# Mixture of experts on one core: all 64 experts in the fixed body, half tiles at other places, five of eight picks read back inside the loop

## The chip, the core and the metric

The kernel runs on one core of a Trainium2 chip. The metric is the device time of one execution in microseconds (us). The engines are TensorE (PE; its weight loads are listed as PEld), VectorE (DVE), ScalarE (ACT), GpSimd (POOL) and SyncE (SP, which here issues the plain DMAs; POOL issues the indirect ones). Each engine runs its own list of instructions in order and waits for the others by semaphores.

## The reference

One transformer block on X of 4 x 512 tokens with D = 512 columns in f32: a modulated layernorm, an attention (linear, without softmax over keys) with a residual, a second modulated layernorm, and a mixture of experts with a residual. The part that the change touches is the mixture. It is, cut to what matters:

```python
logits = x @ gate_w.T                              # 2048 tokens, 64 experts
topv, topi = jax.lax.top_k(logits, 8)
rw = softmax(topv)
W = zeros((N, 64)).at[arange(N)[:, None], topi].set(rw)
gu = einsum('nh,eih->nei', x, gu_w)                # gate and up: 512 -> 2 x 128
gate, up = gu[..., :128], gu[..., 128:]
inter_w = silu(gate) * up * W[:, :, None]
out = einsum('nei,ehi->nh', inter_w, dp_w)         # down: 128 -> 512, summed over experts
out = out + sigmoid(x @ sh_gate1_w.T) * shared_expert(x)
x = x + gb * out                                   # gb: a gate per batch entry
```

So each of 2048 tokens picks 8 of 64 experts, 16,384 pairs of a token and an expert, 256 an expert on average. The kernel computes an expert only on the tokens that picked it.

## The kernel before, in words

The first part (layernorms, attention, shared expert, routing) ends at about 360 us. In it POOL writes, by indirect DMA, for each expert the list of its pairs; the list of all experts lies in memory as `slots` and is read back into the table `tbl` (`load_table`): one column is the 128 pairs of one tile.

**The loop over experts.** The work is in tiles of 128 gathered tokens. Every expert has two fixed tiles (FIXED = 2). What an expert has beyond 256 tokens goes into half tiles of 64 rows; two halves, mostly of two experts, make up one tile of the kind `rest` (18 of them, `REST`). The order is written out by hand in `BODY` (L72 on), a list of tiles: experts 1 to 56 with two tiles each, and a half-tile pair after the tile numbers in `REST_AFTER` (after experts 11, 13, 15, 18 and so on, about every two and a half experts, up to expert 53). Experts 57 to 64 (`LISTED = 8`) are not in the body but in `laps` of four experts: two laps always (`OWN_LAPS`), more in a hardware loop if the routing needs them. In a lap the number of the expert and the column of the table are read from lists in memory (`plan`) on SP (`load_listed`), ACT (`own_listed`), DVE (`list_listed`) and POOL (`gather_listed`). 112 + 18 + 16 = 146 tiles are computed.

A `unit` is an expert's two tiles or one tile of halves. For each unit, in this order:

- SP loads the expert's weights, 768 KB, into one of four slots (`WSLOTS = 4`, `fixed_w`), when the down matmuls of the expert four earlier are done (`after_down`, L624). The weights of a tile of halves go into their own two slots (`rest_w`): gate and up 2 x 512 KB after the gate and up of the tile of halves before (`load_rest_gu`, L566; `next_rest_gu`, L617), down 2 x 256 KB after its down (`load_rest_down`).
- POOL gathers the 128 rows of the tile from memory (indirect DMA, L766, `gather`), eight tiles ahead, and after each gather scatters the results of the tile two earlier to `y_rows` (L775, `put_rows`), a row for each pair. Ids of a tile of halves come from DVE (`list_rest`, L1432: for each half it reads a column number from memory and copies the column).
- PE transposes the gathered rows of the next unit (L2016, `turn`), does gate and up (L2026, `gate_up`; halves L2037, `gate_up_rest`), and then the down matmuls of the unit before (L2046; halves two units later, L2054). ACT copies the transposed rows (L1006) and applies silu (L1016, halves L1014). DVE multiplies (the gating, L1622, halves L1620) and scales the results by the token's weight (L1641).
- In the first units DVE and PE also plan: they count the tokens of each expert, lay out the halves and write the lists (`plan_step` on PE, `take_over` to `plan_listed` on DVE, `lists`). DVE turns parts of the table into gather ids with `list_fixed` when it comes to tiles 6, 10 and 12.

**The final stage.** For each token the eight rows of `y_rows` are summed, scaled by gb and added to x. There are 16 groups of 128 tokens. Picks are sorted by expert, so a token's last picks in the order of the row are done earliest. Two picks (`EARLY = 2`) are read in the last lap (`read_early`, L663). The other six (`LATE = 6`) are read in halves of three rows, 768 KB each (`read_back`, L670), into five buffers (`BACK = 5`); the first ones that need all scatters go out after the last scatter has landed. PE sums four of the six late rows by matmuls with the identity into a bank (`late_row`, L2134; `BY_PE = 4`), DVE adds the other two (`late_pair`, L1703), the two early ones to each other (`early_pair`, L1699), then the bank's sum (L1718), scales (L1719) and adds to x (L1720), and SP stores the group.

## Time and profile before

| | |
|---|---|
| median of 3 runs | 967.36 us (964.57 to 973.53) |
| span of the profiled execution | 965.6 us |
| PE busy | 872.5 us (90%) |
| DVE busy | 465.5 us (48%) |
| POOL busy | 458.7 us (48%) |
| ACT busy | 214.3 us (22%) |
| moved by DMA | 221.36 MB, mean 229 GB/s |
| mean granted clock of PE | 0.970 of full speed |

The runs and the profile are different executions of the same kernel; the median stands 1.8 us above the span of the profiled one. The span is from the first to the last instruction. Busy shares are means over stages with different limits: PE is at nine tenths and more from about 430 us to the end of the loop, DVE is busiest in routing and in the final stage, and DMA moves more than 300 GB/s in most of the loop and about 400 in the final stage.

### The profile page before, as it was taken

The numbers are of one execution on the slowest core, as the hardware profiler recorded it, in microseconds if no ns is written. First come the engines' busy times: TensorE is split into PE (matmuls) and PEld (weight loads), VectorE is DVE, ScalarE is ACT, GpSimd is POOL, SyncE is SP. The second block draws the span as 40 slices with busy tenths as digits, with TensorE's granted clock in tenths as the row PEclk, the third lists the DMA queues.
The fourth block names the chain that finished last, engine by engine and source line by source line (L and its number), as shares of the span: only waits on it lengthen the run. The fifth ranks groups of instructions, "written<-read, shape, count | busy, mean of one in ns | idle before, by whom it ended". The sixth has DMA issues, their size and how long they took to land.

```text
span 965.6 us, 12358 instructions
## 1 busy us (share of the span) xinstructions
PE 872.5 (90%) x3437; PEld 514.2 (53%) x3437; DVE 465.5 (48%) x1177; ACT 214.3 (22%) x559; POOL 458.7 (48%) x447
## 2 busy tenths in 40 slices
PE   6999989989988694979989998999999999986997
PEld 2434534534534343657666665666666666763442
DVE  4797785788586540423323323333233333324496
ACT  2022221321312111212232222322223222321000
POOL 1420055236355766357556666566665656655000
PEclk9999999999998697989999999999999999998999
DMA  9951003103003152788898998889998997899997
GB/s 341 326 163 71 1 8 96 45 2 104 1 1 115 41 190 73 229 289 277 289 322 272 339 323 315 307 286 338 325 319 302 311 333 262 283 354 402 382 419 315
DMA packets 76927, 221.36 MB, mean 229 GB/s; under 512 B 19078, under 2 KB 19462, under 8 KB 76472
## 3 DMA queue, kind: packets, MB, share of 16 engines
q1 hardware_dynamic: 48760, 149.12, 43.9%
q0 software_dynamic: 28096, 71.42, 21.0%
q8 instruction: 29, 0.48, 0.2%
q14 instruction: 42, 0.34, 0.1%
HBM read 183.98 MB, written 48.87 MB: 241 GB/s over the span
## 4 chain that ended last, share of the span: by engine, by line
PE 60%; issue 8%; DVE 7%; another core or an unknown queue 7%; DMA 4%; SPq 3%; ACT 2%; ACTq 0%; POOL 0%; DVEq 0%; POOLq 0%
PE bank L2026 17%; PE bank L2046 8%; PE bank L1798 7%; PE bank L2016 5%; PE bank L1845 5%; PE bank L1911 3%; PE bank L2136 3%; DMA front<-y_rows 3%; PE bank L2037 2%; PE bank L1809 2%; SPq L668 2%; PE bank L2054 1%; PE bank L1930 1%; DMA front<-h_rows,gid_fixed 1%
## 5 line engine op out<-in xcount | busy, mean ns | idle before, releaser
L2026 PE MATMUL bank<-h2T,wqkv 128*128 128x256 f32 x1024 | 243.1, 388 | 9.9 <-issue 9.6
L719 POOL DMA_INDIRECT slot_table<-pair,place x128 | 130.4, 1019 | 183.3 <-DVE place L1262 118.2
L2026 PEld LDWEIGHTS bank<-h2T,wqkv 128*128 128x128 f32 x1024 | 193.1, 194 | 41.1 <-issue 16.5
L775 POOL DMA_INDIRECT y_rows<-front,tbl x110 | 113.6, 1033 | 83.8 <-DVE front L1641 38.1
L766 POOL DMA_INDIRECT front<-h_rows,gid_fixed x112 | 115.8, 1034 | 69.1 <-issue 31.6
L2046 PE MATMUL bank<-wqkv,front 128*128 128x512 f32 x256 | 127.9, 621 | 11.2 <-DVE front L1622 7.5
L1641 DVE TENSOR_SCALAR front<-bank,wgt 128x512 f32<-128x512 f32 x146 | 107.1, 748 | 43.3 <-DMA y_rows<-front,tbl 19.8
L1006 ACT ACTIVATE h2T<-bank 128x512 f32<-128x512 f32 x148 | 82.2, 595 | 161.4 <-issue 65.6
L1798 PE MATMUL bank<-wqkv,front 128*128 128x512 f32 x256 | 113.5, 594 | 0.0
L1622 DVE TENSOR_TENSOR front<-bank,front 128x256 f32<-128x256 f32 x64 | 27.2, 424 | 177.4 <-ACT front L1016 135.2
L2016 PEld LDWEIGHTS bank<-const,front 128*128 128x128 f32 x592 | 69.1, 143 | 62.0 <-issue 47.4
L2016 PE MATMUL bank<-const,front 128*128 128x128 f32 x592 | 81.6, 277 | 22.3 <-ACT h2T L1006 10.3
L2046 PEld LDWEIGHTS bank<-wqkv,front 128*128 128x128 f32 x256 | 44.2, 191 | 70.5 <-issue 33.5
L1798 PEld LDWEIGHTS bank<-wqkv,front 128*128 128x128 f32 x256 | 47.6, 190 | 55.9 <-issue 55.1
L1620 DVE TENSOR_TENSOR front<-bank,front 128x128 f32<-128x128 f32 x18 | 5.3, 292 | 113.3 <-ACT front L1014 96.2
L1845 PE MATMUL bank<-front 128*128 128x512 f32 x128 | 56.6, 594 | 2.5 <-DVE front L1252 2.4
L1809 PE MATMUL bank<-front,wqkv 128*128 128x512 f32 x128 | 58.2, 599 | 0.0
L1016 ACT ACTIVATE front<-bank 128x256 f32<-128x256 f32 x64 | 24.2, 378 | 143.5 <-PE bank L2026 64.5
L2136 PE MATMUL bank<-front,const 128*128 128x512 f32 x100 | 47.2, 622 | 6.9 <-DMA front<-y_rows 6.6
L1845 PEld LDWEIGHTS bank<-front 128*128 128x128 f32 x128 | 23.8, 190 | 31.5 <-issue 29.4
L1809 PEld LDWEIGHTS bank<-front,wqkv 128*128 128x128 f32 x128 | 23.6, 190 | 30.5 <-issue 30.5
L2136 PEld LDWEIGHTS bank<-front,const 128*128 128x128 f32 x100 | 19.3, 199 | 34.1 <-issue 20.8
(292 smaller groups left out, 860.1 us busy)
## 6 DMA issues: line engine op xcount, KB each, us to landing
wqkv<-in_experts SPq DMA_DIRECT2D x64, 768.0 KB
front<-in_experts SPq DMA_DIRECT2D x36, 512.0 KB
front<-y_rows SPq DMA_DIRECT2D x20, 768.0 KB, 12.4
front<-in_experts SPq DMA_DIRECT2D x36, 256.0 KB
wqkv<-y_rows SPq DMA_DIRECT2D x12, 768.0 KB, 13.4
front<-in_w_mod SPq DMA_DIRECT2D x5, 1024.0 KB, 10.1
x<-in_x SPq DMA_DIRECT2D x4, 1024.0 KB, 10.8
h_rows<-h SPq DMA_DIRECT2D x4, 1024.0 KB
```

The lines of the kernel that those rows point to most:

```text
L719: pool.indirect_dma_start(out=slots[:, :], out_offset=bass.IndirectOffsetOnAxis(ap=place[b % 2][:, i, k:k + 1], axis=0), in_=pair[:, b * T ...
L766: pool.indirect_dma_start(out=xg[s], out_offset=None, in_=h2_rows[:, :], in_offset=bass.IndirectOffsetOnAxis(ap=of, axis=0), bounds_check= ...
L775: pool.indirect_dma_start(out=y_rows[:, :], out_offset=bass.IndirectOffsetOnAxis(ap=to, axis=0), in_=yb[s], in_offset=None, bounds_check=P ...
L1006: sc.activation(xT[u % 2][:, :, i * P:(i + 1) * P], bank[n % 2][:, :].rearrange("p (k t) -> p k t", k=KC), ACT.Copy).then_inc(s_xT, 1)
L1641: ve.tensor_scalar(yb[n % YBUFS], bank[4 + n % 2][:, :], wgt[:, n % ROUND:n % ROUND + 1], None, ALU.mult).then_inc(s_y, 1)
L1798: mm = pe.matmul(bank[2 + j][:, :], hT[:, k, i * P:(i + 1) * P], win[:, k, (j + 1) * D:(j + 2) * D], start=(k == 0), stop=(k == KC - 1))
L1809: mm = pe.matmul(bank[4 + c % 2][:, :], win[:, k, c * P:(c + 1) * P], hT[:, k, :], start=(k == 0), stop=(k == KC - 1))
L1845: mm = pe.matmul(bank[4 + i % 2][:, :], qT[:, k, i * P:(i + 1) * P], woa[:, k, :], start=(k == 0), stop=(k == KC - 1))
L2016: mm = pe.transpose(bank[n % 2][:, k * P:(k + 1) * P], xg[n % ROUND][:, k * P:(k + 1) * P], ident)
L2026: mm = pe.matmul(pair_bank[u % 2][:, j * PAIR:(j + 1) * PAIR], w[:, at:at + INNER], xT[u % 2][:, k, :], start=(k == 0), stop=(k == KC - 1))
L2046: pe.matmul(bank[4 + n % 2][:, :], inter[u % RING][:, i * P:(i + 1) * P], w[:, KC * GU:WROW], start=True, stop=True).then_inc(s_d, 1)
L2136: return pe.matmul(sum_bank[g % BACK][:, :], ident, back[g % BACK][k], start=(k == BY_PE - 1), stop=(k == BY_PE - 2))
```

## The change

**Order and slots.** All 64 experts are in `BODY`; the laps and their lists are gone. The 18 tiles of halves come after experts 13, 15, 17, 19 and so on, every second expert but for two steps of three, up to expert 49. The first nine experts have weight slots of their own, from the tenth on seven slots are used in turn; slots 8 and 9 become the weights of the halves. SP, going through the tiles in order, loads the next expert into the slot just freed before it loads the gate and up of the next halves.

**Halves' ids and weights.** POOL reads the ids of the halves from `slots` in memory with 18 more indirect DMAs (`take_ids`, 128 addresses each), two each at tiles 10 to 12 and one each at tiles 13 to 24, ahead of that turn's scatter and gather. The scatter of a turn now stands before its gather. DVE shifts the ids for the gather in two instructions (`list_rest`), no longer column by column, and picks the halves' weights of the tokens with one instruction per tile (`weight_picked`); ACT takes the weights of fixed tiles alone (`weights_of`). The planning steps compute addresses instead of lists. A limit for each expert (`C_LIMIT`) keeps a half tile from coming later than the read-back of its pick.

**Early rows.** Five picks (`EARLY = 5`) are read inside the loop, in chunks of four groups (`read_chunk`, 4 x 256 KB), from the points at which experts 43, 50, 55, 58 and 60 are done. The first pick's rows go to 16 buffers, those of the next four to a ring of three chunks, and DVE adds them (`add_next`): 52 adds at fixed places in the loop, the last 12 in the final stage (`add_last`).

**What does not fit.** If an expert's halves find no place, or a token's pick comes later than its early read, a loop at the end computes that expert again or anew and reads the early rows again (`used > 0`); before, the laps took these.

**Final stage.** Three late rows are read per group, in one DMA of 768 KB, into seven buffers (`BACK = 7`). PE sums two of them, DVE adds the third (`add_late`).

A wait of POOL for gate and up of the shared expert (`s_shg`) goes, the buffers of gathered rows and of the shared expert lie elsewhere, and constants change with the plan.

```diff
-WSLOTS = 4
+WSLOTS = 7
+FIRST_SLOTS = 9
...
-REST_AFTER = [22 + 2 * (42 * m // 17) for m in range(REST)]
+REST_AFTER = [13 + (36 * m) // 17 for m in range(18)]
+REST = len(REST_AFTER)
+PLACES = 2 * REST
+MOST = 4
+SLOT_AT = [q * WROW for q in range(FIRST_SLOTS - 1)] + [12 * WROW]
...
+for e in range(1, EXPERTS + 1):
+    BODY += [(e, 0), (e, 1)]
+    if e in REST_AFTER:
+        BODY.append((None, len(SINGLE)))
+        SINGLE.append(REST_AFTER.index(e))
...
+def slot_of_expert(e):
+
+    return e - 1 if e <= FIRST_SLOTS else (e - FIRST_SLOTS - 1) % WSLOTS
...
+SOON = 5
+EARLY_UPTO = [43, 50, 55, 58, 60]
+EARLY = len(EARLY_UPTO)
+EARLY_TILES = [BODY.index((e, 1)) + 1 for e in EARLY_UPTO]
...
 LATE = TOPK - EARLY
-BY_PE = 4
+CHUNK = 4
+CHUNKS = TILES // CHUNK
+ECHUNKS = 3
+CHUNK_AT = [EARLY_TILES[0] + 1 + 3 * i for i in range(CHUNKS)]
+CHUNK_AT += [EARLY_TILES[1] + 1 + 2 * i for i in range(CHUNKS)]
+CHUNK_AT += [EARLY_TILES[2] + 1 + 2 * i for i in range(CHUNKS)]
+CHUNK_AT += [EARLY_TILES[3] + 2 + i for i in range(2 * CHUNKS)]
+assert CHUNK_AT == sorted(CHUNK_AT)
+ADDED = (EARLY - 1) * CHUNKS - ECHUNKS
+BACK = 7
...
+ID_FIRST = 6
+ID_AT = [10 + n // 2 for n in range(ID_FIRST)] + [7 + n for n in range(ID_FIRST, REST)]
+LIST_REST_AT = [next(u for u in range(UNITS) if UNIT[u][0] >= t) for t in (17, 7 + REST + 4)]
...
+        rest_w = fixed_w[WSLOTS:]
+
+        back = [w.rearrange("p (k d) -> p k d", k=LATE) for w in fixed_w[:BACK]]
...
+            def read_chunk(j):
+                k, c = j // CHUNKS, j % CHUNKS
+                landed_upto(sp, EARLY_TILES[k])
+                if k:
+                    n = j - CHUNKS
+                    if n >= ECHUNKS:
+                        sp.wait_ge(s_added, CHUNK * (n - ECHUNKS + 1))
+                    for i in range(CHUNK):
+                        sp.dma_start(next_row[CHUNK * (n % ECHUNKS) + i], y_view[CHUNK * c + i, :, TOPK - 1 - k, :]).then_inc(s_next[n % ECHUNKS], 16)
+                else:
+                    for i in range(CHUNK):
+                        sp.dma_start(early[CHUNK * c + i], y_view[CHUNK * c + i, :, TOPK - 1, :]).then_inc(s_first, 16)
...
+            for t in range(BODY_TILES):
                 e, n = BODY[t]
-                sp.wait_ge(s_d, t + 1)
-                if e is None:
-                    if n + 1 < REST:
-                        load_rest_down(n + 1)
-                elif e + WSLOTS < FIRST_LISTED:
-                    load_fixed(e + WSLOTS)
-                else:
-                    sp.wait_ge(s_plan, 2)
-                    load_listed(e + WSLOTS - FIRST_LISTED, (e - 1) % WSLOTS)
-
-            for u in range(BODY_UNITS + 1):
-                if u in REST_UNIT:
-                    next_rest_gu(u)
-                if u - 2 in REST_UNIT:
-                    after_down(UNIT[u - 2][0])
-                if u > 3 and u - 1 not in REST_UNIT:
-                    after_down(UNIT[u - 1][1])
-
-            def slot_free(r, q):
-                sp.wait_ge(s_d, listed_tile(r, FIXED * (q + 1)))
+                if e is not None and n == 1:
+                    if next_in_slot(e):
+                        sp.wait_ge(s_d, t + 1)
+                        load_fixed(next_in_slot(e))
+                    if e == FIRST_SLOTS:
+                        sp.wait_ge(s_d, t + 1)
+                        sp.wait_ge(s_addr, 2)
+                        load_rest_gu(0)
+                        load_rest_down(0)
+                if t in REST_TILE[:-1]:
+                    n = REST_TILE.index(t)
+                    sp.wait_ge(s_G, REST_UNIT[n] + 1)
+                    load_rest_gu(n + 1)
+                    sp.wait_ge(s_d, t + 1)
+                    load_rest_down(n + 1)
+                for j in range(EARLY * CHUNKS):
+                    if CHUNK_AT[j] == t:
+                        sp.wait_ge(s_d, t + 1)
+                        read_chunk(j)
...
+            def read_back(g):
+                sp.dma_start(back[g % BACK], y_view[g, :, 0:LATE, :]).then_inc(s_fl[g % BACK], 16)
+
+            for q in range(FIRST_SLOTS):
+                sp.wait_ge(s_ws[q], 16 * SLOT_USES[q])
             for g in range(BACK):
-                read_back(g, 0)
-                refill_second(BACK + g)
+                read_back(g)
             for g in range(TILES):
+                sp.wait_ge(s_fo, g + 1)
                 if g + BACK < TILES:
-                    sp.wait_ge(s_ft, g + 1)
-                    read_back(g + BACK, 0)
-                sp.wait_ge(s_fo, g + 1)
+                    read_back(g + BACK)
...
+            def take_ids(n):
+                pool.indirect_dma_start(
+                    out=sid_rest[:, n:n + 1], out_offset=None, in_=slots[:, :],
+                    in_offset=bass.IndirectOffsetOnAxis(ap=addr[:, n:n + 1], axis=0),
+                    bounds_check=P * EXPERTS * SLOT_COLS - 1, oob_is_err=False).then_inc(s_scat_last[2 if n < ID_FIRST else 3], 16)
...
-            pool.wait_ge(s_shg, KEPT + 1)
...
-                if t != STORE_BACK:
-                    gather_body(t + ROUND)
+                if t == ID_AT[0]:
+                    pool.wait_ge(s_addr, 1)
+                    for b in range(2):
+                        pool.wait_ge(s_scat[b], 16 * TOPK * TPB * (2 - b))
+                    for i in range(len(PICKS)):
+                        pool.wait_ge(s_scat_last[i], 16 * TPB * len(PICKS[i]))
+                for n in range(REST):
+                    if ID_AT[n] == t:
+                        take_ids(n)
                 if t >= STORE_BACK:
-                    put_body(t - STORE_BACK)
-                if t == STORE_BACK:
-                    gather_body(t + ROUND)
-
-            def lap(r):
-                for j in range(ROUND):
-                    gather_listed(r, j + ROUND)
-                    put_listed(r, j - STORE_BACK)
+                    put_rows(t - STORE_BACK)
+                if t + ROUND < BODY_TILES:
+                    gather(t + ROUND)
+            for t in range(BODY_TILES - STORE_BACK, BODY_TILES):
+                put_rows(t)
...
+            def weights_of(u):
+
+                if u in SINGLE_UNIT:
+                    return
                 for t in UNIT[u]:
-                    own_body(t)
-                silu(u, 0)
...
-            def list_rest(n):
-
-                if n == 0:
-                    ve.wait_ge(s_rest, 2)
-                    ve.wait_ge(s_swapped, 16 * len(HALVES))
-                for h in HALVES:
-                    col = ve.value_load(rest[0:1, 0, 2 * n + h:2 * n + h + 1], min_val=0, max_val=DUMMY_COL)
-                    ve.tensor_scalar(gid_rest[rows_of(h), n:n + 1], tbl[rows_of(h), bass.ds(col, 1)], TOPK.bit_length() - 1, None,
-                                     ALU.logical_shift_right)
-                    ins = ve.tensor_copy(sid_rest[rows_of(h), n:n + 1], tbl[rows_of(h), bass.ds(col, 1)])
-                ins.then_inc(s_lists, 1)
...
+            def list_rest(i):
+
+                a, b = ((0, ID_FIRST), (ID_FIRST, REST))[i]
+                ve.wait_ge(s_scat_last[2 + i], 16 * TPB * len(PICKS[2 + i]) + 16 * (b - a))
+                ve.tensor_scalar(gid_rest[:, a:b], sid_rest[:, a:b], TOPK.bit_length() - 1, None,
                                  ALU.logical_shift_right).then_inc(s_gid, 1)
...
+            def weight_picked(u):
+                t = UNIT[u][0]
+                s, n = t % ROUND, BODY[t][1]
+                ve.wait_ge(s_xg[s], 16 * (t // ROUND + 1))
+                if n:
+                    ve.wait_ge(s_picked, n)
+                of = base[:, n:n + 1]
+                ve.scalar_tensor_tensor(out=picked[:, :], in0=const[:, C_PICK:C_PICK + EXPERTS], scalar=of,
+                                        in1=xg[s][:, D:XW], op0=ALU.is_equal, op1=ALU.mult,
+                                        accum_out=wgt[:, s:s + 1]).then_inc(s_picked, 1)
...
+            def add_next(m):
+                n, g = m // CHUNK, m % TILES
+                if m % CHUNK == 0:
+                    ve.wait_ge(s_next[n % ECHUNKS], 16 * CHUNK * (n // ECHUNKS + 1))
+                if m == 0:
+                    ve.wait_ge(s_first, 16 * TILES)
+                if m >= TILES:
+                    ve.wait_ge(s_added, m - TILES + 1)
+                ve.tensor_tensor(early[g], early[g], next_row[m % (CHUNK * ECHUNKS)], ALU.add).then_inc(s_added, 1)
+
+            ADD_AT = [CHUNK_AT[CHUNKS + m // CHUNK] + SOON + m % CHUNK // 2 for m in range(CHUNK * ADDED)]
...
+                if u in LIST_REST_AT:
+                    list_rest(LIST_REST_AT.index(u))
+                taken(u)
+                while added < CHUNK * ADDED and ADD_AT[added] <= UNIT[u][-1]:
+                    add_next(added)
+                    added += 1
...
-            def late_pair(g):
-                part = back[g % BACK]
-                ve.wait_ge(s_fl[g % BACK][1], 16 * (g // BACK + 1))
-                step(tf, ve.tensor_tensor(part[4], part[4], part[5], ALU.add))
-                ve.tensor_tensor(early[0][g], early[0][g], part[4], ALU.add).then_inc(s_pre, 1)
...
+            def add_late(g):
+                if g in paired:
+                    ve.wait_ge(s_v, paired[g])
+                ve.wait_ge(s_fl[g % BACK], 16 * (g // BACK + 1))
+                paired[g] = t0.mark(ve.tensor_tensor(early[g], early[g], back[g % BACK][:, LATE - 1, :], ALU.add))
+
+            add_late(0)
             for g in range(TILES):
-                if g + FIRST_SUMS < TILES:
-                    early_pair(g + FIRST_SUMS)
-                ve.wait_ge(s_fm, paired[g])
-                if g >= BACK:
-                    ve.wait_ge(s_pre, g - BACK + 1)
+                ve.wait_ge(s_v, paired[g])
                 ve.wait_ge(s_ft, g + 1)
-                step(tf, ve.tensor_tensor(early[0][g], early[0][g], sum_bank[g % BACK][:, :], ALU.add))
-                step(tf, ve.tensor_tensor(early[0][g], early[0][g], rows_g[:, g // TPB, :], ALU.mult))
-                ve.tensor_tensor(x_at(g), x_at(g), early[0][g], ALU.add).then_inc(s_fo, 1)
-                if g + BACK < TILES:
-                    ve.wait_ge(s_fm, paired[g + BACK])
-                    late_pair(g + BACK)
+                step(t0, ve.tensor_tensor(early[g], early[g], sum_bank[g % BACK][:, :], ALU.add))
+                step(t0, ve.tensor_tensor(early[g], early[g], rows_g[:, g // TPB, :], ALU.mult))
+                ve.tensor_tensor(x_at(g), x_at(g), early[g], ALU.add).then_inc(s_fo, 1)
+                if TILES - CHUNK * ECHUNKS <= g + 3 < TILES:
+                    add_last(g + 3)
+                if g + 1 < TILES:
+                    add_late(g + 1)
...
-                for k in range(BY_PE - 2):
-                    late_row(g, k)
-                late_row(g, BY_PE - 2).then_inc(s_ft, 1)
-                n = g + BACK - 1
-                if BACK <= n < TILES:
-                    pe.wait_ge(s_fo, n - BACK + 1)
-                    late_row(n, BY_PE - 1).then_inc(s_row3, 1)
...
+                pe.wait_ge(s_fl[g % BACK], 16 * (g // BACK + 1))
+                if g >= BACK:
+                    pe.wait_ge(s_fo, g - BACK + 1)
+                for k in range(LATE - 1):
+                    mm = pe.matmul(sum_bank[g % BACK][:, :], ident, back[g % BACK][:, k, :], start=(k == 0), stop=(k == LATE - 2))
+                mm.then_inc(s_ft, 1)
```

## Rows read from the trace of the kernel before

**Rows 1.** Page of the profile: the span.
```profile
span 965.6 us, 12358 instructions
```

**Rows 2.** Stretches: length; PE, PEld, DVE, ACT, POOL busy; clock, DMA share, GB/s.
```profile
431.00:820.00 389.00, 371.66 (x1809) 252.67 (x1808) 122.91 (x281) 102.24 (x319) 235.42 (x228) 1.00 0.88 307
820.00:882.00 62.00, 55.71 (x240) 40.49 (x238) 16.35 (x42) 16.64 (x58) 37.37 (x37) 0.97 0.93 333
...
908.00:965.00 57.00, 49.83 (x112) 20.13 (x111) 48.37 (x73) 0.00 (x0) 0.00 (x0) 1.00 0.93 380
```

**Rows 3.** PE timeline: start us, us; experts (L2026), half tiles (L2037), late sums (L2136).
```profile
362.25 3.62 PE L2026 MATMUL bank<-h2T,wqkv 128*128 128x256 f32 x16
...
498.34 3.62 PE L2026 MATMUL bank<-h2T,wqkv 128*128 128x256 f32 x16
...
517.51 1.95 PE L2037 MATMUL bank<-front,h2T 128*64 128x256 f32 x16
...
534.24 1.95 PE L2037 MATMUL bank<-front,h2T 128*64 128x256 f32 x16
...
818.82 3.62 PE L2026 MATMUL bank<-h2T,wqkv 128*128 128x256 f32 x16
...
824.87 3.62 PE L2026 MATMUL bank<-h2T,wqkv 128*128 128x256 f32 x16
...
873.60 5.41 PE L2026 MATMUL bank<-h2T,wqkv 128*128 128x256 f32 x16 [2.11 <-issue]
...
914.27 3.70 PE L2136 MATMUL bank<-front,const 128*128 128x512 f32 x8 [0.27 <-DVE x L1720]
```

**Rows 4.** DVE timeline: the last experts, then the final stage.
```profile
881.43 0.42 DVE L1622 TENSOR_TENSOR front<-bank,front 128x256 f32<-128x256 f32 x1 [8.74 <-ACT front L1016]
...
888.16 1.29 DVE L1705 TENSOR_TENSOR wo<-wo,bias_kv 128x512 f32<-128x512 f32 x2
...
908.10 0.69 DVE L1718 TENSOR_TENSOR wo<-wo,bank 128x512 f32<-128x512 f32 x1 [12.63 <-PE bank L2136]
908.82 0.69 DVE L1719 TENSOR_TENSOR wo<-wo,rows_g 128x512 f32<-128x512 f32 x1
909.55 0.69 DVE L1720 TENSOR_TENSOR x<-x,wo 128x512 f32<-128x512 f32 x1
910.16 0.68 DVE L1699 TENSOR_TENSOR front<-front 128x512 f32<-128x512 f32 x1
...
911.48 0.68 DVE L1705 TENSOR_TENSOR rows_a<-rows_a,shared_w 128x512 f32<-128x512 f32 x1
...
962.46 0.69 DVE L1720 TENSOR_TENSOR x<-x,rows_b 128x512 f32<-128x512 f32 x1
```

**Rows 5.** POOL timeline: end of its first run, indirect DMAs in a row, last scatter.
```profile
380.47 1.02 POOL L766 DMA_INDIRECT front<-h_rows,gid_fixed  x1 [0.30 <-issue]
...
413.36 1.03 POOL L766 DMA_INDIRECT front<-h_rows,gid_fixed  x1 [6.50 <-DVE gid_fixed L1429]
...
416.02 1.04 POOL L766 DMA_INDIRECT front<-h_rows,gid_fixed  x1 [0.31 <-issue]
...
888.67 1.03 POOL L775 DMA_INDIRECT y_rows<-front,sid  x1 [0.30 <-issue]
```

**Rows 6.** SP timeline: weights of a half tile; first read-backs after the last scatter.
```profile
526.09 1.81 SPq L569 DMA_DIRECT2D front<-in_experts  x2
527.94 0.43 SPq L557 DMA_DIRECT2D wqkv<-in_experts  x1
...
896.70 2.47 SPq L671 DMA_DIRECT2D front<-y_rows  x5
```

**Rows 7.** Read-backs of L671: DMA from issue to landing.
```profile
DMA to landing us min/median/max: 4.8/13.0/17.3
```

**Rows 8.** ACT timeline: activations that began late after their matmuls.
```profile
384.56 0.38 ACT L1016 ACTIVATE front<-bank 128x256 f32<-128x256 f32 x1 [18.31 <-remote]
...
525.35 0.28 ACT L1014 ACTIVATE front<-bank 128x128 f32<-128x128 f32 x1 [5.82 <-remote]
```

987 lines of the change are left out of this document (476 added, 511 removed).

## Prediction

> **What bounds the kernel now.** I read the page first, then the busy time in stretches, then the timelines of TensorE (PE), VectorE (DVE), GpSimd (POOL) and SyncE (SP) where the shares change. The page gives a span of 965.6 us [rows 1]; the question is which PE time the change removes and which waits it takes away. Four stretches matter.
>
> The attention and routing part, up to about 360 us, is touched by the change only in where buffers lie. I cost it at nothing: no operation on its engines changes, and what goes (a wait of POOL for the shared expert's matmuls) had long been met when POOL came to it.
>
> The body of the expert loop runs from about 431 to 820 us with PE busy for 371.7 of 389 us and DMA at 0.88 [rows 2]. One expert (two tiles) starts every 6.05 us there (818.82 to 824.87) [rows 3]. PE bounds it, but DMA and POOL are close behind.
>
> The end of the body and the two listed laps (820 to 882 us) fall off that pace. From 824.87, the seventh expert after that should start 7 x 6.05 = 42.4 us later, at 867.2; it starts at 873.60, after 2.1 us of idle, and takes 5.4 us instead of 3.6 [rows 3]. Its gating on DVE is at 881.43 [rows 4].
>
> The final stage begins when the last scatter has landed: POOL issues that at 888.67 [rows 5], SP's first read-backs that had to wait for it go out at 896.70 [rows 6], the first sum is taken by DVE at 908.10 and the last row is done at 963.15 [rows 4]. DMA is at 0.93 and 380 GB/s in it [rows 2], and read-backs take a median of 13.0 us to land [rows 7]. It is bound by moving six rows per token.
>
> **The change, term by term.** The tiles are the same in number: before, 112 tiles of 56 experts, 18 of two halves each and 16 listed; after, 128 and 18. A count of the reference's routing gives 35 halves for 36 places, never more than 2 for an expert, and no token whose picks come later than the early rows allow, so the repair loop at the end is not entered. PE's work in the loop stays as it is, less two tiles that were turned for nothing.
>
> *A, the laps go: -10.2 us (from -10.2 to -5).* The listed experts become ordinary ones: no expert or column read from memory on ACT, DVE and SP, no ids copied on ACT. At the pace of 6.05 us the last expert would start at 867.2 instead of 873.60: -6.4. From the start of its gate and up to the gating is 7.8 us before; at the ordinary 3.62 us [rows 3] plus about 0.8 for the activation and the gating it is 4.4: -3.4. The unit before 824.87 is 0.4 us long too. If these delays come from the stream of code and not from the laps, half of them stays.
>
> *B, the ids of the half tiles move from DVE to POOL: +5.3 us (0 to +24).* 18 indirect DMAs (take_ids) are added, two each at tiles 10 to 12, one each at tiles 13 to 24. POOL needs 2.66 us for two of them in a row (413.36 to 416.02) [rows 5], so 1.33 each and 24 us in all, at the head of the queue in which each later gather and scatter stands. POOL enters tile 6 at 413.36, since it waits for a list that DVE writes at the same point in both kernels. From there: tiles 6 to 9 at 2.67 to 424.1; 10 to 12 at 5.34 to 440.1; 13 to 24 at 4.0 to 488. PE needs 3.03 us per tile, so it waits for gathers from about tile 20. The gathers of tiles 32 and 33 (expert 16), issued at 487 and 489.8, land by about 493 (3.5 us for 288 KB, an estimate below the 4.8 us of the quickest 768 KB [rows 7]), and expert 16 begins its gate and up after a half tile, a down and a pair of transposes, at about 498. Before, it begins at 498.34 [rows 3]. Level, but three half tiles are done by then before and two after: one more is to come, 5.3 us. The lower end is a POOL that catches up, the upper its 24 us in full. In the same stretch the nine slots bring experts 5 to 9 early, which speeds the gathers, which is in those 3.5 us.
>
> *C, weights of the half tiles: +3 us (0 to +37).* Half tiles now come after every second expert nearly throughout. The matmuls of one end at 519.46 (517.51 + 1.95); the next one begins at 534.24 [rows 3]. SP issues the first weights of the next at 526.09 and the last by 527.9 [rows 6], 6.3 us before they are used; the quickest landing of 768 KB is 4.8 us [rows 7]. After the change SP loads the next expert first: 768 KB more ahead in the queue are 2.6 us at 307 GB/s [rows 2], and 0.5 us to issue. That is up to 2.3 us late, sixteen times over 37. When SP sees its signals early the load is gone before, and each wait stretches the cycle and so relieves DMA. I take a few of them.
>
> *D, last gating to the first read-back: -1.3 us (-5 to +5).* Before: 881.43 to 896.70, 15.3 us [rows 4, 6]. After: the eight adds of the last unit (8 x 0.61, the start-to-start of an add without a wait, 909.55 to 910.16 [rows 4]) stand ahead of the last two outputs: these are done 8 us after the gating instead of 4, the last scatter goes out at 10, and with a queue that is nearly empty (no expert is loaded in the last seven units) it lands by 13; 14 with SP's code. The other 44 adds (27 us) lie in a DVE that is idle for two thirds of the loop [rows 2]; if they did not, each waiting add would hold the gating behind it, and PE after it.
>
> *E, the final stage: -8.0 us (-19 to +5).* Before: 896.70 to the end, 68.9 us. After: three rows per token instead of six, 16 x 768 KB + 4 MB of output = 16.8 MB, 44 us at 380 GB/s, so DMA no longer bounds it. DVE does. Bank sum, scaling and the add to x take 2.06 us (908.10 to 910.16); the late row 0.71 and the last early row 0.61 (910.16 to 911.48 holds one of each kind) [rows 4]. Groups 1 to 12 have all five: 12 x 3.38 = 40.6; three have 2.77; the last 2.1: 50.9 us. Before it the first read lands and two rows are summed by PE, 7.5 us (before 11.4); behind it 2.4 us for the last store, as now (963.15 to 965.6). 60.9 us. The lower end is the DMA's bound, the upper a PE at 1.2 GHz, the lower of its two levels: four sums take 3.70 us at full clock [rows 3], so the two of a group take 1.9 and would take 3.7, longer than DVE's 3.38.
>
> *Sum:* -10.2 + 5.3 + 3 - 1.3 - 8.0 = -11.2 on 965.6: a span of 954.4. The median of the runs (967.36) stands 1.8 above this span, so the forecast is 956.
>
> **A rule weighed.** Two DVE adds of two SBUF operands take 1.29 us from 888.16 on, beside POOL's last indirect DMA, and one takes 0.68 at 910.16, with POOL idle [rows 4]; that indirect DMA of 888.67 takes 1.03 us as at 413.36 [rows 5]: in this trace neither delays the other. The Trainium skill (GPSIMD Engine Reference, Specifications) says that GpSimd shares its SBUF interface with VectorE and contends with DVE instructions that have two SBUF inputs. The 52 new adds in the loop are of that form. By the row the sum stays; by the rule it grows as in rival 4.
>
> **The rivals.**
> 1. *Half tiles wait for weights (the other side).* The place is the gate and up of each of 16 half tiles, the price 2.3 us each, 37 us in place of C's 3: 990; a third of that already takes the gain. It decides from the point where the next expert's load is still in the queue when the half's goes in. For it: the late issue at 526.09, 6.6 us after the matmuls [rows 6]. Against it: PE shows no wait for such weights now, and slower cycles ask less of DMA. As a whole I take 975 to 990.
> 2. *Signals of PE held up by POOL.* ACT begins at 384.56 what PE had finished at 365.9, and POOL's run of indirect DMAs had ended at 381.5; a later one comes 5.8 us late at 525.35 [rows 3, 5, 8]. The releaser is unknown. Term B makes POOL's run 75 us long. Two holds like the first, less 6 us each that PE covers, are +25: 981.
> 3. *POOL's ids are free and the final stage is quick.* B at 0, E with buffers ahead of DVE: 956 - 5 - 6 = 945.
> 4. *POOL and DVE hold each other up.* If each of the 52 adds in the loop stopped POOL for its 0.61 us, POOL would lose 32 us over the last 40 tiles, where it needs 2.67 us of PE's 3.03 and has 14 us to spare: +18, 974. Against it: the equal durations of [rows 4, 5].
> 5. *The repair loop is entered after all*, 80 rows read again: 20 MB at 380 GB/s are 55 us, and its copies: over 1010. The count of the routing excludes it.
>
> **How the numbers follow.** Forecast 0.46, rival 1 0.15, 2 0.10, 3 0.20, 4 0.06, small remainders between. A measurement of this kernel can tell about 1% (9.7 us) from no change. The forecast lies just past that bound, and half of its own spread of +-8 us on each side of it; with rival 3 that makes 0.47 for faster; 0.31 for the same; 0.22 for slower. The range 938 to 978 takes in B to D at a third of their upper ends, and leaves out the ends of rivals 1 and 2.
>
> **What would show it.** Right: 146 tiles, no instruction of the repair loop; the last gate and up about 1 us or more before 873; between its gating and the first read-back 14 us; in the final stage DVE busy without gaps at 3.4 us a group and DMA well under 0.9. B right: POOL without a pause from 413 to about 488 and PE waiting for gathers from tile 20. C wrong or right: PE's waits at the half tiles' matmuls. The forecast is wrong if PE waits there at all regularly, if an ACT stall as at 366 appears in POOL's long run, or if the final stage turns out to wait for DMA or for PE's sums.

## The result, and the profile after

The changed kernel takes 1021.6 us (median of 4 runs, 1018.45 to 1029.59) where the kernel before takes 966.76: a ratio of 1.058 (95% interval 1.052 to 1.063). The forecast was 956, faster. The page and the busy time in stretches of the changed kernel (columns as in [rows 2]):

```profile
span 1021.8 us, 11572 instructions
PE 861.8 (84%) x3353; PEld 515.5 (50%) x3353; DVE 483.0 (47%) x1161; ACT 203.9 (20%) x503; POOL 477.5 (47%) x458
...
431.00:518.00 87.00, 68.90 (x274) 45.97 (x273) 18.31 (x36) 14.96 (x44) 55.12 (x54) 0.86 0.62 205
518.00:846.00 328.00, 290.54 (x1362) 194.81 (x1361) 87.25 (x182) 68.88 (x201) 175.46 (x171) 0.95 0.83 288
846.00:937.00 91.00, 84.95 (x387) 63.12 (x386) 47.34 (x78) 24.02 (x73) 57.48 (x50) 1.00 0.98 367
...
960.00:1022.00 62.00, 32.20 (x64) 12.58 (x64) 50.07 (x76) 0.00 (x0) 0.00 (x0) 0.80 0.75 271
```

PE's busy time is 11 us less than before and its idle time much more: in the body it was busy 371.7 of 389 us [rows 2], now 68.9 of 87 us to expert 16, and 290.5 of 328 us to expert 50. To compare kernels whose half tiles stand at different places I use one measure, the **excess**: the start of an expert's gate and up, less 362 us, less 6.05 us for each expert and 5.3 us for each half tile before it. Level excess means PE's pace of before.

| kernel | expert 8 | 16 | 50 | 64 | span |
|---|---|---|---|---|---|
| before | 27.5 | 29.7 | 27.4 | 35.1 | 965.6 |
| after | 27.3 | 55.5 | 92.1 | 98.4 | 1021.8 |

The starts behind it, from PE's timeline of the changed kernel (start, duration; L2053 is an expert's gate and up, L2065 a half tile's):

```profile
518.84 3.62 PE L2053 MATMUL bank<-h2T,store 128*128 128x256 f32 x16
...
610.71 1.95 PE L2065 MATMUL bank<-store,h2T 128*64 128x256 f32 x16
...
615.28 3.62 PE L2053 MATMUL bank<-h2T,store 128*128 128x256 f32 x16
...
621.99 5.34 PE L2053 MATMUL bank<-h2T,store 128*128 128x256 f32 x16 [2.27 <-issue]
...
936.93 3.40 PE L2053 MATMUL bank<-h2T,store 128*128 128x256 f32 x15
```

Expert 16 starts at 518.84 with two half tiles done (before: 498.34 with three [rows 3]), expert 64 at 936.93 instead of 873.60. So 28 us go between experts 8 and 16, and 36.6 between 16 and 50, which is 2.3 us for each of 16 cycles of two experts and a half tile (a cycle takes 17.4 us at PE's pace of before). The line of 621.99 shows a cycle: the second expert after the half tile begins after 2.3 us of idle, and takes 5.3 us where 3.62 is usual. From the start of the last gate and up to the end of the span it is 84.9 us where it was 92.0: there the change brought 7.1.

What POOL does in that cycle, then PE's last transposes (L2043) and ACT:

```profile
609.57 1.03 POOL L821 DMA_INDIRECT y_rows<-ksin,sid_rest  x1 [4.55 <-DVE ksin L1637]
...
620.26 1.03 POOL L821 DMA_INDIRECT y_rows<-ksin,tbl  x1 [0.30 <-issue]
...
622.75 1.03 POOL L807 DMA_INDIRECT store<-h_rows,gid_fixed  x1 [1.46 <-issue]
...
629.98 1.03 POOL L821 DMA_INDIRECT y_rows<-kcos,sid_rest  x1 [6.20 <-DVE kcos L1637]
```

```profile
614.41 1.04 PE L2043 MATMUL bank<-const,store 128*128 128x128 f32 x8
...
618.34 0.60 ACT L1040 ACTIVATE h2T<-bank 128x512 f32<-128x512 f32 x1 [4.12 <-remote]
621.25 0.60 ACT L1040 ACTIVATE h2T<-bank 128x512 f32<-128x512 f32 x1 [2.31 <-remote]
624.21 0.38 ACT L1050 ACTIVATE store<-bank 128x256 f32<-128x256 f32 x1 [2.19 <-remote]
```

POOL stands 4.6 to 6.2 us at the scatter of a half tile, whose result DVE has not scaled yet, with the next gather behind it. Then it issues nine indirect DMAs 0.3 us apart (609.57 to 621.3). ACT copies at 618.34 and 621.25 two tiles whose transposes PE had done by 615.5, and PE's idle of 2.3 us waits for the second copy. This is the pattern of rival 2 [rows 8]. The gate and up behind the idle stretch runs at a granted clock of 0.72 (622 to 628 us), hence its 5.3 us.

### The profile page after: what moved, and what is told of

It is laid out like the page before. It is cut to its first block, busy times and chain, and to the rows that moved or that the text cites. A ratio compares the mean times of both kernels' runs of the same rounds, so it can differ in the third digit from the quotient of the medians.

```text
span 1021.8 us, 11572 instructions
## 1 busy us (share of the span) xinstructions
PE 861.8 (84%) x3353; PEld 515.5 (50%) x3353; DVE 483.0 (47%) x1161; ACT 203.9 (20%) x503; POOL 477.5 (47%) x458
## 3 DMA queue, kind: packets, MB, share of 16 engines
q0 software_dynamic: 28032, 71.42, 20.1%
## 4 chain that ended last, share of the span: by engine, by line
PE 55%; issue 12%; DVE 10%; another core or an unknown queue 8%; DMA 4%; POOL 2%; ACT 1%; POOLq 0%; DVEq 0%; SPq 0%; ACTq 0%
PE bank L2053 17%; PE bank L2074 8%; PE bank L1826 7%; PE bank L2043 5%; PE bank L1873 5%; PE bank L2065 3%; DMA store<-h_rows,gid_fixed 3%; PE bank L1837 2%; POOL y_rows L821 2%; PE bank L2083 1%; PE bank L1958 1%; PE bank L1899 1%; PE bank L1939 1%; DMA y_rows<-kcos,tbl 1%
## 5 line engine op out<-in xcount | busy, mean ns | idle before, releaser
L2053 PE MATMUL bank<-h2T,store 128*128 128x256 f32 x1024 | 262.6, 412 | 27.4 <-issue 23.7
L2053 PEld LDWEIGHTS bank<-h2T,store 128*128 128x128 f32 x1024 | 208.3, 209 | 64.4 <-issue 34.3
L807 POOL DMA_INDIRECT store<-h_rows,gid_fixed x128 | 134.4, 1050 | 75.9 <-issue 51.7
L2074 PE MATMUL bank<-store 128*128 128x512 f32 x256 | 127.9, 621 | 4.4 <-DVE ksin L1637 4.0
L1826 PE MATMUL bank<-store 128*128 128x512 f32 x256 | 113.7, 595 | 0.0
L2043 PE MATMUL bank<-const,store 128*128 128x128 f32 x584 | 83.8, 281 | 33.7 <-DMA store<-h_rows,gid_fixed 17.2
L2043 PEld LDWEIGHTS bank<-const,store 128*128 128x128 f32 x584 | 69.0, 144 | 75.8 <-issue 53.2
L821 POOL DMA_INDIRECT y_rows<-kcos,tbl x66 | 70.3, 1065 | 50.5 <-DVE kcos L1637 29.6
L821 POOL DMA_INDIRECT y_rows<-ksin,tbl x62 | 69.4, 1119 | 36.9 <-issue 16.5
L2074 PEld LDWEIGHTS bank<-store 128*128 128x128 f32 x256 | 44.9, 192 | 63.2 <-issue 32.8
L1826 PEld LDWEIGHTS bank<-store 128*128 128x128 f32 x256 | 47.5, 190 | 56.2 <-issue 54.9
L1637 DVE TENSOR_SCALAR kcos<-bank,wgt 128x512 f32<-128x512 f32 x74 | 54.5, 747 | 17.4 <-PE bank L2074 7.8
L1873 PE MATMUL bank<-store 128*128 128x512 f32 x128 | 56.6, 594 | 2.5 <-DVE store L1258 2.4
L1837 PE MATMUL bank<-store 128*128 128x512 f32 x128 | 58.8, 603 | 0.0
L2184 PE MATMUL bank<-store,const 128*128 128x512 f32 x64 | 32.2, 653 | 27.1 <-DMA store<-y_rows 27.1
```

The source lines that it names most:

```text
L807: pool.indirect_dma_start(out=xg[s], out_offset=None, in_=h2_rows[:, :], in_offset=bass.IndirectOffsetOnAxis(ap=of, axis=0), bounds_check= ...
L821: pool.indirect_dma_start(out=y_rows[:, :], out_offset=bass.IndirectOffsetOnAxis(ap=to, axis=0), in_=yb[s], in_offset=None, bounds_check=P ...
L1637: ve.tensor_scalar(yb[t % YBUFS], bank[4 + t % 2][:, :], wgt[:, t % ROUND:t % ROUND + 1], None, ALU.mult).then_inc(s_y, 1)
L1826: mm = pe.matmul(bank[2 + j][:, :], hT[:, k, i * P:(i + 1) * P], win[:, k, (j + 1) * D:(j + 2) * D], start=(k == 0), stop=(k == KC - 1))
L1837: mm = pe.matmul(bank[4 + c % 2][:, :], win[:, k, c * P:(c + 1) * P], hT[:, k, :], start=(k == 0), stop=(k == KC - 1))
L1873: mm = pe.matmul(bank[4 + i % 2][:, :], qT[:, k, i * P:(i + 1) * P], woa[:, k, :], start=(k == 0), stop=(k == KC - 1))
```

## The experiments

The excess in each, for reading on (b_ kernels are the kernel before with an edit, a_ the changed one, c_ the changed one with several). Each was run beside the kernel before on the same chip, and chips differ: the kernel before took 959 us on two of them and 968 to 971 on the others. "Before" is its median beside that kernel, and the ratio is of the medians or close to it. So kernels from different chips are compared by the ratio, not by their times.

| kernel | expert 8 | 16 | 50 | 64 | span | before | ratio to before |
|---|---|---|---|---|---|---|---|
| b_ids | 30.4 | 56.6 | 53.7 | 61.8 | 990.6 | 967.9 | 1.027 |
| b_put_first | 30.3 | 32.6 | 43.9 | 58.0 | 988.5 | 970.7 | 1.024 |
| a_sp_order | 34.1 | 62.4 | 102.0 | 108.9 | 1032.3 | 967.9 | 1.066 |
| a_gather_first | 27.8 | 55.1 | 63.7 | 66.6 | 990.5 | 967.9 | 1.028 |
| a_ids_spread | 32.2 | 40.5 | 83.6 | 87.3 | 1010.7 | 967.9 | 1.046 |
| a_gf_spread | 30.8 | 37.1 | 71.1 | 72.4 | 998.0 | 970.7 | 1.029 |
| a_small_adds | 29.5 | 58.1 | 94.6 | 100.5 | 1023.4 | 970.7 | 1.053 |
| a_drain | 33.4 | 72.7 | 87.3 | 102.9 | 1027.0 | 968.1 | 1.064 |
| a_gf_drain | 29.3 | 74.6 | 85.4 | 100.8 | 1026.3 | 968.1 | 1.062 |
| a_gf_drain3 | 28.6 | 57.0 | 50.4 | 51.9 | 979.0 | 959.1 | 1.022 |
| b_drain | 29.9 | 30.2 | 43.0 | 57.7 | 989.8 | 968.1 | 1.024 |
| b_head_drain | 26.1 | 25.7 | 18.3 | 30.2 | 959.6 | 959.1 | 0.999 |
| c_sp_ids | 26.3 | 65.9 | 67.3 | 68.3 | 995.3 | 959.0 | 1.039 |
| c_sp_spread | 27.4 | 29.6 | 42.2 | 43.6 | 969.5 | 959.1 | 1.014 |
| c_best | 34.3 | 34.5 | 35.8 | 38.5 | 964.9 | 970.5 | 0.993 |

The loop of b_head_drain is that of the kernel before. On its chip the excess falls by 7.4 us between experts 16 and 50; in the first table it fell by 2.3.

**One part of the change at a time.** The ids alone, in the kernel before: 18 indirect DMAs of 128 ids, into a buffer that nothing reads.

```diff
+                for n in range(REST):
+                    if ID_AT[n] == t:
+                        take_ids(n)
```

> The kernel before with one part of the change alone: 18 more indirect DMAs of 128 single ids on POOL, two each at tiles 10 to 12 and one each at tiles 13 to 24, into a buffer that nothing reads. Theory 1 (the ids' 24 us of POOL make PE wait for gathers and are not caught up): 15 to 28 us slower than before, all of it lost between 430 and 520 us. Theory 2 (the price of that stretch, 28 us in the changed kernel, comes from the order put before gather or from the half tiles' new places, and the 18 DMAs cost the 5 us of my term B): 3 to 8 us slower.

25.5 us slower (993.33 against 967.86; interval of the ratio 1.024 to 1.030), and nearly all of it between experts 8 and 16. In the turn in which POOL gathers tile 32 it is 25.4 us later than in the kernel before (496.30 for 470.89). The order on POOL alone, in the kernel before:

```diff
-                if t != STORE_BACK:
-                    gather_body(t + ROUND)
                 if t >= STORE_BACK:
                     put_body(t - STORE_BACK)
-                if t == STORE_BACK:
-                    gather_body(t + ROUND)
+                gather_body(t + ROUND)
...
                 for j in range(ROUND):
+                    put_listed(r, j - STORE_BACK)
                     gather_listed(r, j + ROUND)
-                    put_listed(r, j - STORE_BACK)
```

> The kernel before with one part of the change alone: in each turn of POOL the scatter ahead of the gather. Theory 1 (the order makes POOL stand at each half tile's result and then issue a long run of indirect DMAs, in which PE's signals come late): 10 to 30 us slower than before, spread over the cycles with half tiles, POOL's waits for DVE before L775 longer. Theory 2 (the order only hurts beside the closer half tiles of the change): within 5 us of before.

23 us slower (1.024, 1.014 to 1.035), spread over the loop; some 6 of them come between experts 50 and 64; the laps, turned round as well, are experts 57 to 64. And undone in the changed kernel:

```diff
+                if t + ROUND < BODY_TILES and t != STORE_BACK:
+                    gather(t + ROUND)
                 if t >= STORE_BACK:
                     put_rows(t - STORE_BACK)
-                if t + ROUND < BODY_TILES:
+                if t == STORE_BACK:
                     gather(t + ROUND)
```

> The changed kernel with one thing undone on POOL: in each turn the gather stands before the scatter again. Theory 1 (the scatter in front, waiting for its result, blocks the gather behind it, in the stretch of the ids above all): 5 to 20 us faster than the changed kernel. Theory 2 (gathers eight tiles ahead have time enough): within 3 us.

994.9 us, 27 less than the changed kernel: the excess stays level from expert 16 to 44 (55.1 to 56.1, where it rose from 55.5 to 83.7), so the order makes the 2.2 us that each cycle lost up to there. Of the 36.6 us up to expert 50 the last 8.6 stay. What the order brought was more than either theory gave.

**The rival on the weights.** SP's order undone in the changed kernel:

```diff
+                    if t + 1 in REST_TILE[:-1]:
+                        m = REST_TILE.index(t + 1)
+                        sp.wait_ge(s_G, REST_UNIT[m] + 1)
+                        load_rest_gu(m + 1)
                     if next_in_slot(e):
                         sp.wait_ge(s_d, t + 1)
...
                     n = REST_TILE.index(t)
-                    sp.wait_ge(s_G, REST_UNIT[n] + 1)
-                    load_rest_gu(n + 1)
```

> The changed kernel with one thing undone on SP: gate and up of the next halves are loaded before the next expert again. Theory 1 (the 2.3 us that each of the 16 cycles of two experts and a half tile lost are a wait for the halves' weights): 25 to 40 us faster than the changed kernel. Theory 2 (they come from PE's signals that reach ACT and DVE late while POOL issues a long run of indirect DMAs): within 5 us of the changed kernel, and PE still idle 2.2 us before the gate and up of the second expert after each half tile.

1031.8 us, 10 more than the changed kernel, though the intervals of the two ratios overlap (1.060 to 1.072 and 1.052 to 1.063). Theory 1 falls; that it was no faster but rather slower, by 6 to 7 us already at experts 1 and 8, was foreseen by neither.

**Ids spread, without and with the order undone.** DVE's shift is made for each tile alone; the second kernel has the edit of a_gather_first besides.

```diff
-ID_AT = [10 + n // 2 for n in range(ID_FIRST)] + [7 + n for n in range(ID_FIRST, REST)]
+ID_AT = [max(10, SINGLE_TILE[n] - 16) for n in range(REST)]
```

> The changed kernel with the same 18 DMAs of ids spread out: each 16 tiles before its half tile, that is one every five tiles, from tile 10 to about 100. Theory 1 (crowding at tiles 10 to 24): 15 to 25 us faster than the changed kernel, excess at expert 16 down from 55 to about 35 us. Theory 2 (any indirect DMA more on POOL costs its 1.3 us wherever it stands): within 5 us of the changed kernel, the loss only moved to later experts.

> The changed kernel with the gather ahead of the scatter again and the 18 DMAs of ids spread over tiles 10 to 100, both together. If the two are separate causes (order: 27 us, crowding: 9 to 17 us), the time is 975 to 985 us. If they are one (a POOL that is behind), the spread adds under 5 us to what the order brings: 990 to 995 us.

1012.3 and 998.75 us. Alone, spreading saves 15 us at expert 16 and keeps 11 at 64. With the gather first it saves 18 at expert 16 and has lost them by 50, and the ratio is that of a_gather_first (1.029 and 1.028): there a DMA more on POOL costs about its 1.3 us wherever it stands. The two edits share their effect and do not add up; I take both for one matter, a POOL that is behind.

**Adds of DVE beside POOL.** The kernel leaves the other 508 columns out of 52 of the adds.

```diff
-                ve.tensor_tensor(early[g], early[g], next_row[m % (CHUNK * ECHUNKS)], ALU.add).then_inc(s_added, 1)
+                ve.tensor_tensor(early[g][:, 0:4], early[g][:, 0:4], next_row[m % (CHUNK * ECHUNKS)][:, 0:4], ALU.add).then_inc(s_added, 1)
```

> The changed kernel with the 52 adds in the loop cut to 4 of 512 columns; the other columns of the early rows are left out of the sum. Theory 1 (two-source adds of DVE and POOL's indirect DMAs hold each other up: the 1.50 and 4.30 us that indirect DMAs take at 938 to 945 us in the changed kernel): these go back to 1.03 us and the last gating to first read-back from 17.1 to 13 us or less; in all 6 to 12 us faster than the changed kernel. Theory 2 (they are independent): only the gating that stood behind adds comes earlier, 1 to 3 us.

1021.7 us (ratio 1.053, the changed kernel 1.058, intervals overlapping): no change that can be told. POOL's timeline of the changed kernel, then of a_small_adds, at a scatter near the end of the loop:

```profile
944.51 4.30 POOL L821 DMA_INDIRECT y_rows<-ksin,tbl  x1 [3.36 <-DVE ksin L1637]
```

```profile
945.76 0.98 POOL L821 DMA_INDIRECT y_rows<-ksin,tbl  x1 [3.49 <-DVE ksin L1637]
```

The adds do hold up indirect DMAs: from 878 us on sixteen of them take 1.26 to 1.50 us and this one 4.30, and in a_small_adds none in the loop takes more than 1.2. But from the last gating to the first read-back it is 17.7 us without them (943.86 to 961.60) and 17.1 with them.

**Are PE's signals held by POOL?** Two measurements behind the last store of the kernel before. In the first, PE's transposes and ACT's copies take turns while POOL gathers:

```diff
+            for n in range(24 * 6):
+                if n:
+                    pe.wait_ge(m_A, TILES + n)
+                for k in range(KC):
+                    mm = pe.transpose(bank[0][:, k * P:(k + 1) * P], ident, ident)
+                mm.then_inc(m_T, 1)
```

> The kernel before with a measurement behind its last store: PE does four transposes and signals, ACT copies the bank and signals back, 24 times in each of six sections: (1) alone, (2) beside 16 indirect gathers of POOL in a row, (3) beside 16 with a pause for landing after every four, (4) as 2 beside 12 expert loads of SP, (5) beside 12 loads alone, (6) beside 16 gathers and 30 two-source adds of DVE. Theory 1 (a long run of indirect DMAs holds PE's signals): a turn of 1.3 to 1.6 us in 1 and 5, single turns of 3 us and more in 2 and 4, fewer in 3. Theory 2 (it takes the traffic of weights too): late only in 4. Theory 3 (neither; the loop's late signals have another source): even turns in all. In section 6, if DVE and POOL share a port, gathers of over 1.03 us.

Even turns of 1.80 us in all sections but for one of 2.55 at the end of the first run: 16 gathers in a row hold nothing that shows, if PE waits for ACT after each four transposes. The sixth section shows what the adds of DVE do to POOL. Its timeline, at the last add:

```profile
1200.25 1.50 POOL L885 DMA_INDIRECT front<-h_rows,gid_fixed  x1 [0.30 <-issue]
1202.05 1.01 POOL L885 DMA_INDIRECT front<-h_rows,gid_fixed  x1 [0.30 <-issue]
```

Ten gathers beside 30 adds take 1.50 us each, the six behind them 1.01. The adds are not slower for it (30 in 18.15 us). For the held signals PE was then kept busy:

```diff
+            for n in range(16 * 4):
+                if n >= 2:
+                    pe.wait_ge(m_A, TILES + n - 1)
+                for k in range(KC):
+                    mm = pe.transpose(bank[n % 2][:, k * P:(k + 1) * P], ident, ident)
+                mm.then_inc(m_T, 1)
+                for k in range(8):
+                    pe.matmul(bank[2 + n % 2][:, 0:GU], const[:, 0:P], h2[:, 0, 0:GU], start=(k == 0), stop=(k == 7))
```

> The kernel before with a measurement behind its last store, PE busy this time: 64 times four transposes and a signal for ACT, which copies the bank, and then eight matmuls of 256 columns; 16 times alone, 16 beside 40 indirect gathers of POOL in a row, 16 beside the next 40 and 20 expert loads of SP, 16 beside 20 loads alone. Theory 1 (PE's signals are late when POOL issues a long run and PE is busy): ACT's copy begins 0.2 us behind the transposes in the first section and 2 to 6 us behind in some of the second and third. Theory 2 (traffic): late in the third and fourth. Theory 3: even in all; then the late signals of the loop have a cause that neither the run nor the loads make.

The four sections in stretches of m_busy (alone; 40 gathers in a row; 40 gathers and 20 loads; loads), and ACT's timeline in the second:

```profile
963.00:1015.00 52.00, 52.00 (x268) 45.81 (x268) 0.00 (x0) 8.36 (x14) 0.00 (x0) 1.00 0.00 1
1019.00:1075.00 56.00, 31.06 (x122) 22.24 (x122) 0.00 (x0) 2.39 (x4) 40.22 (x40) 0.71 0.69 201
1116.00:1180.00 64.00, 64.00 (x330) 56.40 (x329) 0.00 (x0) 9.55 (x16) 37.17 (x37) 1.00 1.01 398
1185.00:1242.00 57.00, 57.00 (x293) 50.22 (x293) 0.00 (x0) 8.96 (x15) 0.00 (x0) 1.00 0.66 266
```

```profile
1025.30 0.60 ACT L1111 ACTIVATE h2T<-bank 128x512 f32<-128x512 f32 x1 [3.30 <-PE bank L2188]
1030.26 0.60 ACT L1111 ACTIVATE h2T<-bank 128x512 f32<-128x512 f32 x1 [4.37 <-PE bank L2188]
1041.63 0.60 ACT L1111 ACTIVATE h2T<-bank 128x512 f32<-128x512 f32 x1 [10.77 <-remote]
1075.29 1.09 ACT L1111 ACTIVATE h2T<-bank 128x512 f32<-128x512 f32 x2 [33.07 <-remote]
```

In the second section PE does 122 matmuls in 56 us, from 1043 us on single ones mostly 1.4 to 2.8 us apart, with nothing in the code for them to wait for, and ACT stands 33 us. The run of gathers (1018.92 to 1071.1) began 11 us before the first late copy and ended 4 before the last. In the third section, with twice the traffic, nothing is late. There POOL has breaks, since it has to wait for a landing before some of its gathers. POOL's timeline of m_busy, third section:

```profile
1124.56 1.00 POOL L883 DMA_INDIRECT front<-h_rows,gid_fixed  x1 [0.68 <-issue]
1126.25 1.00 POOL L883 DMA_INDIRECT front<-h_rows,gid_fixed  x1 [0.69 <-issue]
1128.87 1.00 POOL L883 DMA_INDIRECT front<-h_rows,gid_fixed  x1 [1.61 <-DMA front<-h_rows,gid_fixed]
```

The brackets give the time that POOL stood before each: 0.7 to 1.6 us, where within an unbroken run it is 0.3. So the next kernel puts breaks into the run itself, an iota of one element a lane with a wait for it:

```diff
+                pool.iota(tick[:, :], pattern=[[0, 1]], base=0, channel_multiplier=0).then_inc(s_tick, 1)
+                pool.wait_ge(s_tick, drains[0])
```

> The measurement of m_busy without SP's loads: 16 turns of PE alone, 16 beside 40 indirect gathers of POOL with a tiny iota and a wait for it after each (POOL's sequencer never runs ahead of its engine), 16 beside 40 with that after every fourth, 16 without POOL, 16 beside 40 in a row as in m_busy. Theory 1 (PE is starved when POOL's own queue of indirect DMAs is full without a break): turns of 3.9 us and ACT prompt beside the first 40, prompt or nearly so beside the second, and holds of 5 to 30 us beside the last 40. Theory 2 (it is the descriptors' rate): holds beside all three, the later the slower the rate.

Stretches of m_drain (a break after every gather; after every fourth; none), and ACT in the last:

```profile
1024.00:1086.00 62.00, 62.00 (x321) 54.63 (x320) 0.00 (x0) 9.56 (x16) 28.85 (x49) 1.00 0.39 110
1118.00:1176.00 58.00, 58.00 (x300) 51.17 (x299) 0.00 (x0) 8.96 (x15) 41.24 (x49) 1.00 0.66 185
1224.00:1280.00 56.00, 28.30 (x108) 20.51 (x107) 0.00 (x0) 3.18 (x6) 37.84 (x38) 0.69 0.68 195
```

```profile
1234.02 0.60 ACT L1111 ACTIVATE h2T<-bank 128x512 f32<-128x512 f32 x1 [5.83 <-remote]
1249.64 0.60 ACT L1111 ACTIVATE h2T<-bank 128x512 f32<-128x512 f32 x1 [15.02 <-remote]
1277.79 1.08 ACT L1111 ACTIVATE h2T<-bank 128x512 f32<-128x512 f32 x2 [27.55 <-remote]
```

The hold is there again without a break, and gone with one after every fourth gather. The traffic is not what does it: 185 GB/s of gathers with breaks and 398 with weights hold nothing, 195 without a break do. What is left beside the break itself is POOL's rate, a gather every 1.49 us with breaks and every 1.31 without; no run tells the two apart.

**Breaks in the loop.** The same break, as a function, in every turn of the changed kernel (a_drain), of the changed kernel with the gather first (a_gf_drain), and of the body of the kernel before (b_drain); in the first two it stands behind each DMA of ids too:

```diff
                 if t + ROUND < BODY_TILES:
                     gather(t + ROUND)
+                drain()
```

> The changed kernel with a tiny iota of POOL and a wait for it at the end of every turn of the loop and behind each DMA of ids; nothing else. Theory 1 (late signals behind an unbroken run of indirect DMAs are what order and ids cost): 20 to 50 us faster than the changed kernel. Theory 2 (POOL's throughput is the cost, each instruction more makes it worse): 5 to 20 us slower than the changed kernel.

> The same breaks in POOL's run with the gather ahead of the scatter again. Theory 1: 960 to 975 us, 20 to 35 us faster than a_gather_first. Theory 2: slower than a_gather_first.

> The kernel before with the same break at the end of every turn of POOL's loop. Theory 1: late signals go there too, but PE mostly had cover for them: 0 to 15 us faster than before. Theory 2: 0 to 15 us slower.

1029.2, 1027.6 and 990.65 us. The late signals are gone (between 560 and 800 us ACT's waits put down to "remote" sum to 77 us in the changed kernel and to none in a_drain), and yet none of the three is faster than without breaks, and the last two are clearly slower. The same sum is 70 us in the kernel before: the change did not bring more late signals. POOL's timeline of a_gf_drain shows the price:

```profile
607.28 1.02 POOL L823 DMA_INDIRECT y_rows<-ksin,tbl  x1 [0.30 <-issue]
608.31 0.14 POOL L832 IOTA tick<- 128x1 int32 x1
609.46 1.04 POOL L809 DMA_INDIRECT store<-h_rows,gid_fixed  x1 [1.00 <-POOL tick L832]
610.80 1.02 POOL L823 DMA_INDIRECT y_rows<-kcos,tbl  x1 [0.30 <-issue]
```

A turn is 3.52 us (607.28 to 610.80) instead of 2.67, and five turns are 17.6 us where PE needs 17.4 for a cycle: POOL is the bound. Behind the last half tile, where PE needs 3.03 us a tile, the excess of a_gf_drain rises by 15.4 us up to expert 64, that of a_gather_first by 2.9. With a break in every third turn only, and none behind the ids (against a_gf_drain):

```diff
-                drain()
+                if t % 3 == 2:
+                    drain()
```

> The changed kernel with the gather ahead of the scatter and a break in POOL's run (iota and a wait for it) only in every third turn, none behind the ids. A break costs POOL 0.86 us, 0.29 a turn, so a turn is 2.96 us where it was 2.67 and 3.53 with one each. Theory 1 (breaks cure the hold, and a_gf_drain was slow because POOL at 3.53 us a turn had become the bound): 985 to 1000 us, ACT's late signals at nearly none. If the hold cost much more than throughput: 970 to 985 us. If every 0.3 us a turn on POOL costs in full, over 1005 us.

979.3 us, against 959.1 for the kernel before on this chip: 1.022 (1.014 to 1.029), where a_gather_first had 1.028 (1.022 to 1.035). That is 6 to 7 us less, and the intervals overlap. The excess falls by 6.7 us from expert 16 to 50, where without breaks it rose by 8.6, but on this chip it falls by 7.4 in the loop of the kernel before too (b_head_drain), so some 10 of these 15 us are left. The breaks cost nothing and probably give back some; that the hold costs time in the loop is not shown clear of noise. And ahead of the loop of the kernel before, in the run of [rows 8] (besides, a break behind its gathers):

```diff
-                for k, n in order[first:last]:
+                for m, (k, n) in enumerate(order[first:last]):
                     put_pair(LAST, n, k, s_scat_last[i])
+                    if m % 4 == 3:
+                        drain()
```

> The kernel before with breaks only in POOL's run ahead of the loop (352 to 381 us: the last scatters of the routing and the first gathers), in which ACT began at 384.56 what PE had finished at 365.9. Theory 1 (the hold): ACT is prompt, expert 3 starts up to 10 us earlier, the time is 0 to 10 us less, as far as the lists for experts 4 to 8 do not gate PE anyway. Theory 2 (PE waits for the lists in any case): within 4 us of before although expert 3 starts earlier.

958.35 against 959.08 us (0.997 to 1.002): no difference. The hold is gone (the activation of 384.56 [rows 8] begins at 368.14, as PE's matmuls end) and expert 3 starts at 387.4 instead of 390.2, so the wait of 18 us costs nothing in the end.

**A version without the causes.** The ids by SP's plain DMAs of 64 ids each instead of POOL's (tiles 7 to 24), gather first:

```diff
-                pool.indirect_dma_start(
-                    out=sid_rest[:, n:n + 1], out_offset=None, in_=slots[:, :],
...
+                for h in HALVES:
+                    at = h * HALF_TILE
+                    g = sp.value_load(half_lane[at:at + 1, n:n + 1], min_val=0, max_val=1)
+                    c = sp.value_load(half_col[at:at + 1, n:n + 1], min_val=0, max_val=EXPERTS * SLOT_COLS - 1)
+                    sp.dma_start(sid_rest[at:at + HALF_TILE, n:n + 1], by_half[:, bass.ds(g, 1), bass.ds(c, 1)].rearrange("l g c -> l (g c)"), allow_slow_non_contiguous=True).then_inc(s_ids[n >= ID_FIRST], 16)
```

> The changed kernel with the gather ahead of the scatter again, and with the halves' ids read by 36 plain DMAs of SP (64 ids each, lane and column from registers) in place of POOL's 18 indirect ones. Theory 1 (each indirect DMA more on POOL costs its 1.3 us because POOL is what the loop waits for, so order and ids are what the change lost): about 25 us less than a_gather_first, 965 to 975 us, no faster than before by more than 1%. Theory 2 (ids cost only where they crowd): the same. If a third cause is left (weights of the last half tiles, 7 us between experts 44 and 48), it stands alone: the excess is flat at 30 us up to expert 40 and rises there.

996.4 us, a ratio of 1.039 and slower than a_gather_first: a half tile waited 8.8 us for its weights behind the ids in SP's queue. SP needs about 2.3 us from one such DMA to the next (503.42 to 505.71), not 1.9; the DMA itself has 0.47 of them, and the two registers loaded from memory for its address 0.71 and 0.27. Spread out (against c_sp_ids):

```diff
-ID_AT = [7 + n for n in range(REST)]
+ID_AT = [max(8 + n, SINGLE_TILE[n] - 18) for n in range(REST)]
```

> As c_sp_ids, but SP reads each half tile's ids 18 tiles ahead of it, two small DMAs every five tiles, not all 36 between tiles 7 and 24, where they took SP 1.9 us each and made a half tile wait 8.8 us for its weights and a scatter 22 us for its ids. Theory (gather first, and no indirect DMA more on POOL, is all that the change lacked): excess flat at 30 to 35 us to expert 44, 965 to 975 us. If SP's added 4 us every cycle delay weights: 975 to 990 us.

972.1 us against 959.1, 1.014 (1.007 to 1.021): of the 5.8% that the change lost, 1.4 are left without its order and ids on POOL. The rest has no single place. The excess is 29.6 at expert 16, 31.8 at 28 and 35.5 at 44, where b_head_drain on the same chip has 25.7, 22.8 and 18.6. PE stands before the gate and up of eight of the 18 half tiles, 16.1 us in all (0.5 to 4.4 each); before the four longest ACT had copied the rows 1.6 us earlier or more, so it is the weights that they wait for. The largest wait stands at the last halves; SP's timeline of c_sp_spread, where L695 reads the first early rows and L668 loads a half tile's gate and up:

```profile
756.18 1.77 SPq L695 DMA_DIRECT2D wo<-y_rows  x4
759.07 1.47 SPq L668 DMA_DIRECT2D store<-in_experts  x2
```

SP stands in front of the first early rows until the scatters have landed, the half tile's weights queue behind it, and PE's gate and up at 766.70 waits 4.4 us (3.6 in the changed kernel, 7.1 in a_gather_first).

Last, c_sp_spread with the break in every third turn and the reads of the early rows five tiles later:

```diff
-CHUNK_AT = [EARLY_TILES[0] + 1 + 3 * i for i in range(CHUNKS)]
+CHUNK_AT = [EARLY_TILES[0] + 6 + 3 * i for i in range(CHUNKS)]
```

> c_sp_spread (gather first, ids by SP and spread), with a break in POOL's run every third turn, and with the four reads of the first early pick five tiles later, so that SP no longer stands waiting for scatters to land while the weights of the last halves are due. Theory: the breaks bring 10 to 14 us as from a_gather_first to a_gf_drain3, the reads 4 to 7 us, from 1.014 of before in c_sp_spread: 0.99 to 1.00 of before. If POOL's 0.29 us a turn costs as much as the hold gives back: 1.005 to 1.015.

963.35 against 970.54 us, a ratio of 0.993 (0.990 to 0.995; 12 and 17 runs): faster than both kernels, by 0.7% than the kernel before. The wait at the last halves is gone; what of the gain from 1.014 is due to the breaks and what to the reads no run separates. Its page and body:

```profile
span 964.9 us, 11973 instructions
...
431.00:820.00 389.00, 365.92 (x1789) 254.06 (x1788) 115.91 (x252) 94.55 (x274) 241.54 (x267) 0.99 0.90 317
```

## Why the prediction was wrong

The difference of the spans is 56.2 us: +63.3 at the start of the last gate and up, -2.1 from there to its gating (5.7 us, was 7.8), +1.8 to the first read-back, -6.8 in the final stage. By my terms:

- **A step that I left out: the scatter ahead of the gather.** It stands in the diff and no term priced it. It is the largest cost, 27 us undone and 23 us added alone. The front of POOL's queue was where I should have asked what is queued behind a waiting instruction: put_rows(t - 2) of a half tile waits for a result two units later, and the gather for tile t + 8 stands behind it. Over eight cycles from 513 to 674 us POOL stands 4.4 to 7.5 us at that result, 5.5 in the mean. With the 13.4 us of its ten DMAs that is more than PE's cycle of 17.4, and a cycle takes 20.1. In the kernel before, from 475 to 700 us, it stands 0.3 to 3.3 us there, and in places 2.4 to 3.4 at a gather whose buffer PE still holds: it is ahead of PE.
- **B, mis-sized: 5.3 us, measured 25.5 alone.** I had POOL's 24 us as the upper end. The step that failed is the timeline, which ends level with the kernel before at expert 16 (498 us). In the run expert 16 begins at 518.84. The timeline has POOL's DMAs and none of its waits for results: POOL was through with the ids at 495 us, not 488, since it came to tile 6 at 416.4 and stood 5.0 and 4.6 us at results (451.63, 479.83). It gives a gather 3.5 us to land, where PE could begin on that of 489.14 at 495.20. And it leaves out what PE loses while it waits: matmuls of 5.98 us for 3.62 and a mean granted clock of 0.86 from 431 to 518 us. Nothing was caught up: in b_ids POOL waits for PE's buffers again from 513.73 on, so from there PE is the bound and keeps its pace, and what it has lost stays lost. Rival 4's room (2.67 of 3.03 us a tile) makes the same mistake: an engine's waits in order are part of its time.
- **C and rival 1: refuted as priced.** The 2.3 us a cycle came out to the tenth, by chance, from another cause; with SP's order undone the kernel is no faster. C's own numbers do not give 2.3 either: the weights had 6.3 - 4.8 = 1.5 us to spare and come 2.6 + 0.5 = 3.1 us later, which is 1.6 late. PE did wait for halves' weights at one place that counts, 3.6 us, behind the reads of early rows, a wait on SP that I had not listed. In c_sp_spread, where POOL no longer holds PE up, such waits are 16.1 us; the ids stand in SP's queue there too, so how many of them are the change's own is open.
- **Rival 2: the mechanism exists, its price here is not shown.** POOL's runs do hold PE's signals, in m_busy and in the cycle above, where PE then idles 2.3 us and goes on at a lower clock. But they are held as much in the kernel before (70 us against 77), breaks in every turn removed them and gave no time back, and breaks in every third turn gave 6 to 7 us that do not stand clear of noise. Nor did two large holds of 12 us appear.
- **Rival 4 and the rule weighed.** The Trainium skill (GPSIMD Engine Reference, Specifications) has GpSimd contend with VectorE for a shared SBUF interface when a VectorE instruction has two SBUF inputs. With indirect DMAs of 1.50 and once 4.30 us beside the adds and 0.98 to 1.01 without, the traces of the changed kernel and of m_signals agree, against my reading of equal durations from one short overlap. The price in total was nothing that can be measured.
- **A, the gain is there once POOL is in order, and smaller.** From expert 50 to 64 the excess rises by 6.3 us after (7.7 before), but by 2.9 in a_gather_first and 2.7 in c_best. From the last gate and up to its gating it is -2.1 for -3.4.
- **D and E.** First read-back 17.1 us after the last gating, not 14: the last scatter went out at 9.7 as forecast, but it took 7.4 us more and not 4. The adds are not the reason: in a_small_adds it is 7.6 (953.99 to 961.60). E gave -6.8 for -8.0, with DVE the bound, a group every 3.4 us once the first bank had come:

```profile
968.34 0.69 DVE L1745 TENSOR_TENSOR wo<-wo,bank 128x512 f32<-128x512 f32 x1 [3.14 <-PE bank L2184]
969.06 0.69 DVE L1746 TENSOR_TENSOR wo<-wo,rows_g 128x512 f32<-128x512 f32 x1
969.78 0.69 DVE L1747 TENSOR_TENSOR x<-x,wo 128x512 f32<-128x512 f32 x1
970.39 0.68 DVE L1739 TENSOR_TENSOR wo<-wo,store 128x512 f32<-128x512 f32 x1
```

Open: how the 2.3 us of a cycle divide between the held signals and POOL's standing alone (a break removes the one and adds to the other), why the loop's excess differs from chip to chip, why a_sp_order and the c_ kernels start expert 1 later (369 to 380 us for 362), and what inside the chip an unbroken run blocks.

## What to carry to other kernels

For an engine that works through one queue in order, count its waits with its work: its work plus the time it stands behind an unfinished result is what must stay under the bounding engine's cycle, and an instruction that will have to wait goes behind those that need not. Price every reordering in a diff, also the one that moves no work. Where GpSimd issues indirect DMAs one after another beside a busy TensorE, look for activations that start late with no releaser on the core, and try a rare break in the run; here a rare one was worth some 0.7%, within noise, and one in every turn cost more than it gave. And compare kernels by the ratio to one that ran beside them: the kernel before alone varied by 1.2% from chip to chip, more than that.

## What was not expected of the hardware

With 40 indirect gathers in a row, 1.31 us apart, a busy PE fell from 5.2 matmuls a us (268 in 52) to 2.2 (122 in 56), its clock was granted at 0.71, and a signal reached ACT up to 38 us after the transposes (m_busy: PE's end at 1036.94, ACT's start at 1075.29). One tiny instruction of POOL with a wait for it after every fourth gather ended this (300 matmuls in 58 us, clock 1.00), and beside weights loads at 398 GB/s, where POOL's gathers had pauses of their own, it did not occur. DVE's adds of two SBUF operands stretched an indirect DMA from 1.01 to 1.50 us.
